# A graph-network chain on one core: attention terms made tile by tile, and three block loads issued a stage earlier

## What is computed

```python
def _gat_conv(x, W, a_src, a_dst, b, src, dst, n):
    xw = x @ W
    e = jax.nn.leaky_relu((xw @ a_src)[src] + (xw @ a_dst)[dst], 0.2)
    m = jax.ops.segment_max(e, dst, num_segments=n)
    ex = jnp.exp(e - m[dst])
    s = jax.ops.segment_sum(ex, dst, num_segments=n)
    alpha = ex / (s[dst] + 1e-16)
    agg = jax.ops.segment_sum(alpha[:, None] * xw[src], dst, num_segments=n)
    return agg + b
```

## Time and profile before

| | us |
|---|---|
| median of 3 runs | 6073.62 (6070.95 to 6088.92) |
| the profiled execution | 6096.4 |
| its span, first to last instruction | 6094.6 |
| PE / DVE / POOL / ACT busy | 5009.5 / 3754.7 / 3033.4 / 1626.2 |
| terms stage | 2988.7 to 3035.3 |
| rows stage | 3035.3 to 3060.6 |
| maxima stage | 3060.6 to 3264.6 |
| attention, norm and early experts stages | 3264.6 to 3886.0 |

### The profile page before, as it was taken

How to read it: one execution, slowest core, us unless ns; L and a number is a source line. 1 busy time by engine, 2 the same in 40 slices (tenths; PEclk the granted TensorE clock), 3 DMA queues, 4 the chain that set the end, 5 groups by cost and what they waited for, 6 DMA issues and landing times.

```text
span 6094.6 us, 70632 instructions
## 1 busy us (share of the span) xinstructions
PE 5009.5 (82%) x23594; PEld 2988.6 (49%) x23658; DVE 3754.7 (62%) x7230; ACT 1626.2 (27%) x2761; POOL 3033.4 (50%) x2051
## 2 busy tenths in 40 slices
PE   5767666665879898989757879888996999999999
PEld 3444444434445575557656556684333333222266
DVE  6698668876676602121224531398996998777744
ACT  2111111112212201220122221126872002666521
POOL 5777888888888887887877886300000000000000
PEclk8777777777899988998878779999998999999999
DMA  7767666675555597559799877894443011323200
GB/s 188 152 136 137 123 129 121 130 102 59 16 11 18 1 124 52 16 7 103 73 180 127 76 46 86 131 221 112 123 112 78 26 29 30 82 80 82 79 11 28
DMA packets 558646, 523.49 MB, mean 86 GB/s; under 512 B 263681, under 2 KB 489925, under 8 KB 557210
## 3 DMA queue, kind: packets, MB, share of 16 engines
q1 hardware_dynamic: 295610, 427.94, 32.5%
q0 software_dynamic: 261696, 90.13, 25.3%
q10 hardware_dynamic: 1028, 1.52, 0.1%
HBM read 365.60 MB, written 153.76 MB: 85 GB/s over the span
## 4 chain that ended last, share of the span: by engine, by line
PE 51%; DVE 21%; DMA 9%; issue 8%; SPq 5%; POOL 5%; ACT 1%; DVEq 0%; ACTq 0%; POOLq 0%; PEldq 0%
PE PS L2431 6%; PE PS L1057 6%; PE PS L2268 5%; PE PS L1029 5%; PE PS L1448 5%; SPq L188 4%; DVE MXS L2309 4%; DVE XT L545 3%; DVE WORK L2072 3%; PE PS L1040 3%; DMA WORK<-x_table,WORK 3%; DVE ROWS L1705 3%; DVE ROWS L545 2%; DMA WORK<-pairs 2%; POOL sums L822 2%
## 5 line engine op out<-in xcount | busy, mean ns | idle before, releaser
L760 POOL DMA_INDIRECT pairs<-PAIR_CNT,PAIR_IDX x1364 | 2154.1, 1579 | 525.6 <-issue 461.2
L545 DVE SCALAR_TENSOR_TENSOR XT<-PS,ROWS 128x1024 f32<-128x1024 f32 (+1 forms) x704 | 694.1, 1049 | 156.4 <-PE PS L515 138.4
L822 POOL DMA_INDIRECT sums<-WORK,XT x340 | 531.0, 1562 | 179.2 <-issue 96.5
L2502 DVE SCALAR_TENSOR_TENSOR WORK<-WORK 125x1000 f32<-125x1000 f32 x400 | 462.2, 1197 | 151.2 <-ACT WORK L2470 150.4
L632 PE MATMUL PS<-WORK,IDENT 125*125 125x256 f32 x680 | 283.0, 507 | 265.4 <-DMA WORK<-x_table,WORK 265.1
L2268 PE MATMUL PS<-ROWS 32*125 32x500 f32 x3200 | 451.0, 633 | 28.9 <-DVE MXS L2309 19.1
L2309 DVE TENSOR_REDUCE MXS<-PS 125x4 f32<-125x2000 f32 x200 | 439.0, 2235 | 24.4 <-PE PS L2289 20.4
L2470 ACT ACTIVATE WORK<-PS 125x1000 f32<-125x1000 f32 x400 | 380.0, 1002 | 237.8 <-PE PS L2419 237.8
L675 ACT ACTIVATE WORK<-PS 125x256 f32<-125x256 f32 x340 | 130.7, 384 | 1167.5 <-PE PS L632 1167.5
L515 PE MATMUL PS<-ROWS 128*128 128x512 bf16 x704 | 244.1, 466 | 225.5 <-DVE XT L545 162.1
L1057 PE MATMUL PS<-WORK 128*125 128x256 f32 x1760 | 409.5, 387 | 3.6 <-ACT WORK L1126 3.6
(11 more groups left out here) (344 smaller groups left out, 7984.4 us busy)
## 6 DMA issues: line engine op xcount, KB each, us to landing
WORK<-pairs SPq DMA_DIRECT2D x400, 218.8 KB
pairs<-ROWS SPq DMA_DIRECT2D x75, 976.6 KB, 7.3
WORK<-pairs SPq DMA_DIRECT2D x48, 1093.8 KB
WORK<-pairs SPq DMA_DIRECT2D x80, 546.9 KB
pairs<-PAIR_CNT,PAIR_IDX POOLq DMA_INDIRECT x1364
WORK<-pairs SPq DMA_DIRECT2D x40, 382.8 KB
XT<-pairs SPq DMA_DIRECT2D x12, 1093.8 KB
mask_t<-ROWS SPq DMA_DIRECT2D x40, 273.4 KB
```

Of the source, the lines that this page charges most:

```text
L545: dve.scalar_tensor_tensor(junk[:, slot:slot + width // SUPER, :].rearrange("p a n -> p (a n)"), PS[:, bank + (0 if both else h):bank + (2 ...
L760: pool.indirect_dma_start(table, bass.IndirectOffsetOnAxis(idx[:, n:n + 1], 0), cnt[:, n:n + 1], None, compute_op=ALU.add).then_inc(sem(do ...
L822: pool.indirect_dma_start(sums[c], bass.IndirectOffsetOnAxis(SROW[:, k:k + 1], 0), SUMMED[:, k % 8, :], None, compute_op=ALU.add).then_inc ...
L2502: dve.scalar_tensor_tensor(E3[q % 8], E3[q % 8], 1.0, A3[n % 4][0:P].unsqueeze(1).to_broadcast([P, 2, CH]), ALU.min, ALU.mult).then_inc(se ...
```

## The change

Two things change. `l2b_dve` works per tile: once tile t is in `Y257`, DVE issues for each of the two rows one instruction over 125 x 256 that multiplies and sums along the row (`accum_out`), so the four instructions over 125 x 5120 become forty small ones. Their products are thrown away into two slots in `ROWS`, no longer into `WORK`. Each waits until the one two before it is complete.

With `WORK` free in that stage, SP issues the loads of the blocks 0, 1 and 2 there. The load of block 3, whose buffer holds `T_W` until the terms stage ends, moves to the start of the maxima stage, ahead of the stores and loads there. The rows stage is now without work for SP.

```diff
-        ATT = flat(WORK, 2048, T, D)
+        ATT = [ROWS[0:P, 6, q * D:(q + 1) * D] for q in range(2)]
...
-            st.step(dve.memset(Y257[:, :, D:AGG], 1.0))
-            dve.wait_ge(sem("l2b_out"), T)
-            for q in range(2):
-                st.step(dve.tensor_tensor(ATT[0:P], Y257[:, :, 0:D], over_tiles(ROW[:, 1 + q, :]), ALU.mult))
-                st.step(dve.tensor_reduce(GAT[q][:, :, 0], ATT[0:P], AX, ALU.add))
+            st.go(dve.memset(Y257[:, :, D:AGG], 1.0))
+            for t in range(T):
+                dve.wait_ge(sem("l2b_out"), t + 1)
+                for q in range(2):
+                    if t:
+                        st.wait(but=1)
+                    st.go(dve.scalar_tensor_tensor(ATT[q], Y257[:, t, 0:D], 1.0, ROW[:, 1 + q, :], ALU.mult, ALU.mult,
+                                                   accum_out=GAT[q][:, t, 0:1]))
+            st.wait()
             stage_end(dve)
...
             table_sp(sp, "l2a", pairs1, "L2_gnn_W2")
+            for m in range(3):
+                nbmax_load(sp, "l2m", [pairs1], m)
             idle(sp)
-            nbmax_ahead(sp, "l2m", [pairs1])
             idle(sp)
+            nbmax_load(sp, "l2m", [pairs1], 3)
             nbmax_sp(sp, "l2m", [pairs1], True)
```

## The result

The changed kernel takes 6036.45 us (median of 5 runs, 6032.27 to 6049.28), and the kernel before, with five runs by then, 6081.3 us (6070.95 to 6088.92). The ratio is 0.9931, interval [0.9915, 0.9947]: 42 us less, twice the 20 us forecast. Nearest to it lies the first rival, "POOL is out of the way" (6037 to 6046).

The account below looks back on a forecast made before the run. The stages bound the kernel, with POOL's additions 17 us behind as a second chain. Stage gains 21.0 + 17.4 - 1 = 37.4 us, of which POOL's chain lets 20 through: 6076.4 profiled, 6053.7 on the median, range 6038 to 6069.

Parts of the forecast that it names:

- the first rival: POOL's disturbances turn out smaller, so the stages' full gain of 28 to 37 us shows, 6037 to 6046; chance 0.12.
- The terms stage: Four DVE instructions, 22.1 us, replaced by forty small ones; only the last tile's two stand behind ACT; gain 21.0 us.
- DVE keeps up: Terms stage: DVE takes 0.5 us per instruction, 1.0 us per tile, while ACT delivers a tile every 1.08 us.
- The rows stage: Without SP's DMAs it ends with ACT, 7.9 us instead of 25.3; gain 17.4 us, perhaps 1.5 more from PE's clock, left out.
- The maxima stage: One more load, block 3 of 1.25 MB; price between -2 and +7.0 us, taken as +1.
- POOL's chain: POOL's additions to the tables, last landing at 3865.7, decide at the second maxima stage; 17.4 of 37.4 us become SP's wait.
- The 5.8 us: Most POOL could lose if the new DVE instructions, with two SBUF inputs, block its port; 1.2 us was taken instead.
- the stages are the bound by only 17 us: Before the second maxima stage, POOL's last landing at 3868.3 against the experts' last store landed at 3885.51.
- The terms of 0.9 and 2.5 us: POOL's added losses beside transfers: 0.9 us from block 3 in the maxima stage, 2.5 us from the early experts stage.
- The second rival: POOL was already the bound or nearly, its margin under 17 us in unprofiled runs; 0 to 14 us saved, 6060 to 6073; chance 0.22.
- The third: Slow new instructions, costly moved transfers or block 3 costing 7 us cut the gain to about 10 us, 6063; chance 0.06.
- the slower case: POOL becomes the bound and stalls more, in the early experts stage; six more long waits give 6093 us; chance 0.05.

Follow-up runs that it names:

- the tiles alone: Changed kernel with the four block loads back in the rows stage, terms still computed tile by tile; ratio 0.9966 against the kernel before, 20.7 us less.
- before again: The kernel before, unchanged, profiled a second time; 859.4 us from the start of the terms stage to the end of POOL's last addition.
- with less and with more for POOL: Kernel before with POOL's last 40 additions left out (ratio 0.9994), and kernel before with 24 more additions at POOL's end (ratio 1.0024).
- the five compared above: Profiles of the kernel before (twice), only loads moved, only terms per tile, and the changed kernel; POOL lost 108, 94, 84, 81 and 80 us.

## Why the prediction was right in direction and half in size

**The terms stage** was right: 21.0 us forecast, 20.7 in the profile, 20.7 us (interval 13 to 28) with the tiles alone. The step "DVE keeps up" held with more room than I gave it: 0.35 us from start to start, not 0.5. I had taken the length of an instruction for the step to the next; before the change L1554, also 0.48 us long, already started every 0.41 us. SP's six DMAs took 15.7 us, not 18.6, and were hidden.

**The rows stage** gave 19.8, not 17.4. The missing 2.4 us are what I had named, put at 1.5 and left out, "for it will turn out to be hidden": PE is warm. It was not hidden.

**The maxima stage**: +1 us was forecast for block 3. In the profiles it took 188.3 to 206.2 us, whichever kernel; nothing of the change can be told in it, neither the +1 nor the bound of 7.

**The attention and norm stages** were taken as unchanged. They took 298.7, 295.5, 300.8 and 295.9 us in the four profiles of kernels with both old stages (before, before again, with less and with more for POOL) and 289.6 to 294.6 us in the seven with one part of the change or both. That is 6 us, without an overlap, in instructions that no edit touched. It is not explained: the granted clock (0.81 to 0.83 against 0.82 to 0.84) and the waits for loads from `pairs` differ a little, and no run tells them apart.

**POOL's chain is the step that failed.** The forecast said that POOL's last addition would have landed at 3865.7, that 17.4 of 37.4 us would turn into a wait of SP, and that 20 would reach the end. L1570's 7.2 us came back: in the changed kernel no addition near the new instructions took over 1.75 us, and three of fourteen took 0.2 more, a loss of 0.6 us where I had 1.2. The 5.8 us that I had worked out from the rule of the Trainium skill (SBUF — State Buffer, "SBUF: two separate sides") were a bound, and 0.6 us lies far under it: the long instructions bear the rule out, the short ones neither refute it nor come near its worst case. The error is in the term before all that, "the stages are the bound by only 17 us". It took POOL's losses in one execution for those of the kernel. They were the largest of the five compared above (80 to 108 us), and the experiment with 24 more additions puts the lead at 30 us, with a landing of 4.3 us already in it. With 30 in place of 17.4 the same sum (plus 7.2, less 1.2, 0.9 and 2.5) gives a saving of 32.6 us, 6041 on the median shown, which is the first rival; with the lead's error of 8 us it reaches the 37 to 40 us that the stages gained. The terms of 0.9 and 2.5 us for additions beside more transfers were not measured apart. The mechanism itself is real: the changed kernel is the one in which both chains meet, as the extra additions show, 44 us more of them costing 45 us. That the two chains come out level is luck: nothing in the change aims at it, and the 42 us were reached because POOL's lead happened to be just long enough.

The second rival pointed the wrong way. It said that unprofiled runs have a smaller lead than the profiled one; they have a larger one. The third and the slower case found nothing.

Both parts of the change were needed for what it gives: 20.7 and 17.6 us alone, 40 to 42 together. What bounds the kernel now at this place is both chains, 2 us apart by the profile and level within 12 us by the timed runs. Fewer additions alone bring nothing: leaving out 40 did not. By the same reading a shorter stage alone should bring little; no run here shows that.

## What to carry to other kernels

When a saving may be swallowed by a second chain, the whole forecast hangs on the lead of one chain over the other, and one profiled execution can give that lead with an error as large as the lead itself (here 15 us, where a second profile gave 27 and the timed runs 30); lengthen the second chain by a known amount and read the lead from what it costs. Here a stage that ended with SP issuing transfers, and one in which DVE waited for all tiles before it started on the first, gave back nearly all of that wait (19.8 and 20.7 us), and PE started the next stage warm. Look for both forms, and for the second chain before counting the gain.

## What the runs showed of the hardware that was not expected

- A VectorE multiply with a sum along the row of 125 x 256 follows the one before it at 0.35 us, less than the 0.41 us at which an instruction of the same kind and shape without a sum runs before the change (eight in 3.25 us at L1554, which has other operands), although its accumulator read of 82 ns is counted apart.
- A POOL addition beside one VectorE instruction of 5.49 us took 5.1 to 5.4 us; beside the forty short ones 1.54 to 1.75.
- The last indirect addition of 128 single counts landed 5.86 us after the start of its instruction, in both kernels where the chain of waits shows it; beside such additions the last store of the experts' outputs landed in 5.1 to 6.4 us (three profiles) instead of 3.0.
